# Two layer norms in a transformer block: the Newton chain for the reciprocal root on VectorE instead of GpSimd

## The reference

```python
def layernorm(x): return (x - mean(x)) / sqrt(var(x) + 1e-5)        # over the 512 features
x = x + tanh(g_xattn) * attention(layernorm(x), ctx, ctx, mask)     # 16 heads of 32, with o_proj
h = layernorm(x); h_prev = h moved one row down
xr = mu_r*h + (1-mu_r)*h_prev;  xk = mu_k*h + (1-mu_k)*h_prev
x = x + tanh(g_ffn) * sigmoid(xr @ W_r.T) * (square(relu(xk @ W_k.T)) @ W_v.T)
```

## Time and profile before

| | |
|---|---|
| three runs | 1274.07, 1276.35, 1281.88 us (median 1276.35) |
| profiled execution, span | 1275.5 us; no time outside the span is given for it |
| TensorE matmul | 1184.9 us busy, 93% of the span |
| VectorE | 956.5 us, 75% |
| ScalarE | 763.2 us, 60% |
| GpSimd | 253.7 us, 20% |
| mean granted TensorE clock | 0.977 of full |
| stage 1, the seam, stage 2 | to about 862 us, to 888 us, to the end |

### The profile page before, as it was taken

The page is one execution under the profiler, slowest core; times in us unless marked ns, Lnnn a source line. Parts: engine busy times, 40 slices in busy tenths (PEclk is TensorE's granted clock), DMA queues, the critical chain, the costliest instruction groups (busy, mean ns, idle before and its releaser), DMA issues.

```text
span 1275.5 us, 25860 instructions
## 1 busy us (share of the span) xinstructions
PE 1184.9 (93%) x7424; PEld 933.5 (73%) x7424; DVE 956.5 (75%) x2011; ACT 763.2 (60%) x1632; POOL 253.7 (20%) x427
## 2 busy tenths in 40 slices
PE   3999899999999989999999999987999999999997
PEld 3777676777767767777676777765878878878886
DVE  5778688688778867868877887879677677777763
ACT  4678677678768867867866886774432433343332
POOL 1030030030012003003002100025433443343441
PEclk9999999999999989999998999987999999999999
DMA  6433332253243343233224332461111211211200
GB/s 216 113 96 80 100 108 61 70 143 79 64 125 89 79 98 91 76 99 106 75 59 134 82 83 59 115 196 52 51 50 64 84 49 49 99 49 49 78 37 34
DMA packets 72685, 109.81 MB, mean 86 GB/s; under 512 B 14864, under 2 KB 23696, under 8 KB 72592
## 3 DMA queue, kind: packets, MB, share of 16 engines
q1 hardware_dynamic: 72592, 108.92, 29.9%
HBM read 41.76 MB, written 16.78 MB: 46 GB/s over the span
## 4 chain that ended last, share of the span: by engine, by line
PE 65%; DVE 12%; issue 12%; POOL 6%; ACT 1%; POOLq 1%; DMA 1%; DVEq 1%; SPq 1%; ACTq 0%
PE bank L525 15%; PE bank L461 14%; PE bank L492 11%; PE bank L537 9%; PE bank L518 8%; PE bank L501 6%; DVE xh L992 3%; POOL newton L1094 2%; DVE neg_s L875 2%; PE bank L507 1%; POOL var_eps L1088 1%; DVE stats L832 1%; DVE pT L881 1%; DVE stats L981 1%; POOL rstd L1095 1%
## 5 line engine op out<-in xcount | busy, mean ns | idle before, releaser
L697 ACT ACTIVATE probs<-neg_s,negmax 128x512 f32<-128x512 f32 x512 | 368.3, 721 | 58.6 <-DVE negmax L875 50.5
L875 DVE CUSTOM_DVE_ANT_0 neg_s<-bank,mask_big 128x512 f32<-128x512 f32 x512 | 346.4, 684 | 63.7 <-PE bank L518 36.0
L525 PE MATMUL bank<-ident,probs 128*128 128x128 f32 x2048 | 320.7, 280 | 21.8 <-ACT probs L697 21.3
L525 PEld LDWEIGHTS bank<-ident,probs 128*128 128x128 f32 x2048 | 245.0, 143 | 82.5 <-ACT probs L697 43.0
L518 PE MATMUL bank<-k_stack,q_stack 96*128 96x512 f32 x512 | 247.8, 484 | 15.3 <-DVE negmax L875 15.3
L881 DVE COPY pT<-bank 128x512 f32<-128x512 f32 x256 | 176.5, 690 | 105.8 <-PE bank L525 104.6
L704 ACT COPY pT<-bank 128x512 f32<-128x512 f32 x256 | 149.2, 583 | 107.9 <-PE bank L525 104.1
L1088 POOL TENSOR_SCALAR var_eps<-mv 128x2 f32<-128x2 f32 (+1 forms) x24 | 16.6, 690 | 661.7 <-DVE mv L839 597.5
L537 PE MATMUL bank<-pT,v_sb 128*32 128x512 f32 x1024 | 118.8, 605 | 0.8 <-issue 0.5
L518 PEld LDWEIGHTS bank<-k_stack,q_stack 96*128 96x128 f32 x512 | 99.5, 195 | 22.3 <-DVE negmax L875 10.8
L697 ACT ACTIVATION_READ_ACCUMULATOR probs<-neg_s,negmax 128x1 f32 x512 | 97.0, 190 | 0.0
(11 more groups left out here) (111 smaller groups left out, 2169.5 us busy)
## 6 DMA issues: line engine op xcount, KB each, us to landing
k_stack<-k_hi SPq DMA_DIRECT2D x256, 64.0 KB, 2.0
q_stack<-q_hi SPq DMA_DIRECT2D x256, 64.0 KB, 2.0
x_rows<-x SPq DMA_DIRECT2D x8, 1024.0 KB, 6.9
cT_raw<-ctxT SPq DMA_DIRECT2D x8, 1024.0 KB, 5.5
k_stack<-k_lo SPq DMA_DIRECT2D x128, 64.0 KB, 2.0
q_stack<-q_lo SPq DMA_DIRECT2D x128, 64.0 KB, 2.0
ctx_dram<-ctx_sb SPq DMA_DIRECT2D x32, 256.0 KB, 2.1
c_raw<-ctx_dram SPq DMA_DIRECT2D x16, 512.0 KB, 4.2
```

Source lines behind the costliest of these rows:

```text
L525: mm = nc.tensor.transpose(pt_bank[i % 2][:, a * P:(a + 1) * P], probs[:, i % P_RING, a * P:(a + 1) * P], ident[:])
L697: nc.scalar.activation(probs[:, i % P_RING, :], neg_s[:, i % SM_RING, :], ACT.Exp, bias=negmax[:, k:k + 1], scale=-1.0, accum_out=den[:, g ...
L875: nc.vector.tensor_tensor_reduce(neg_s[:, i % SM_RING, :], s_bank[i % S_BANKS][:], mask_big[:, q, :], 1.0, 3e38, ALU.add, ALU.min, negmax[ ...
```

## The change

`inverse_root` goes from GpSimd's list to VectorE's, with the same 15 links in the same form, and is called at the end of `mean_and_variance` and of `residual1`, behind a wait for the last variance. GpSimd's `normalise` waits for the end of the chain and then writes the rows; `normalise(0)` and `inverse_root2` are gone from its list. VectorE waits at its very start until GpSimd has preset the counters. No tile, matmul or DMA changes.

```diff
         @block.vector
+            def inverse_root(base, sem_, var, ve, y, t):
+                n = [0]
+                def link(ins):
+                    n[0] += 1
+                    ins.then_inc(sem_, 1)
+                    dve.wait_ge(sem_, base + n[0])
+                    apart(dve)
+                link(nc.vector.tensor_scalar(ve, var, EPS, None, ALU.add))
+                link(nc.vector.tensor_scalar(t.bitcast(I32), ve.bitcast(I32), -0.5, RSQRT_MAGIC, ALU.mult, ALU.add))
+                link(nc.vector.tensor_copy(y, t))
+                for _ in range(NEWTON):
+                    link(nc.vector.tensor_tensor(t, y, y, ALU.mult))
+                    link(nc.vector.tensor_tensor(t, t, ve, ALU.mult))
+                    link(nc.vector.tensor_scalar(t, t, -0.5, 1.5, ALU.mult, ALU.add))
+                    link(nc.vector.tensor_tensor(y, y, t, ALU.mult))
...
             def mean_and_variance(b):
...
+                dve.wait_ge(mv_done, b * TT + TT)
+                apart(dve)
+                inverse_root(b * CHAIN, rstd_chain, mv[:, :, 1], var_eps[:], rstd[:], newton[:])
...
+            dve.wait_ge(counters_set, 1)
             for t in range(TT):
                 row_stats(0, t)
...
             def residual1(b, h):
...
+                dve.wait_ge(mv2_done, u * UM + UM)
+                apart(dve)
+                inverse_root(u * CHAIN, rstd_chain2, mv2[:, :, 1], var_eps2[:], rstd2[:], newton2[:])
...
         @block.gpsimd
+            pool.sem_inc(counters_set, 1)
             def normalise(b):
-                pool.wait_ge(mv_done, (b + 1) * TT)
+                pool.wait_ge(rstd_chain, (b + 1) * CHAIN)
                 apart(pool)
-                inverse_root(b * CHAIN, pool_chain, mv[:, :, 1], var_eps[:], rstd[:], newton[:])
...
-            normalise(0)
...
-            def inverse_root2(b, h):
-                u = b * 2 + h
-                pool.wait_ge(mv2_done, (u + 1) * UM)
-                apart(pool)
-                inverse_root(u * CHAIN, pool_chain2, mv2[:, :, 1], var_eps2[:], rstd2[:], newton2[:])
             def step2(b, h):
                 u = b * 2 + h
-                if not (h and is_last(b)):
-                    inverse_root2(*((b, 1) if h == 0 else (b + 1, 0)))
...
             split_w2(1)
-            inverse_root2(0, 0)
             split_w2(2)
```

More of the change, by code:

```diff
@@ L209, in build @@
         small_ld, bias_ld, bv_ld = sem("small_ld"), sem("bias_ld"), sem("bv_ld")
-        unused = sem("unused")
+        unused, counters_set = sem("unused"), sem("counters_set")
         ident_ld = sem("ident_ld")
@@ L217, in build @@
         x_ld, c_ld = sem("x_ld"), sem("c_ld")
-        bn_done, mv_done, pool_chain, xhat_done = sem("bn_done"), sem("mv_done"), sem("pool_chain"), sem("xhat_done")
+        bn_done, mv_done, rstd_chain, xhat_done = sem("bn_done"), sem("mv_done"), sem("rstd_chain"), sem("xhat_done")
         side_mm, side_hi, side_done = sem("side_mm"), sem("side_hi"), sem("side_done")
@@ L229, in build @@
         o_mm, x1_done, bn2_done, mv2_done = sem("o_mm"), sem("x1_done"), sem("bn2_done"), sem("mv2_done")
-        pool_chain2, xh_done, t_mm, xT_done, carry_done = (
-            sem("pool_chain2"), sem("xh_done"), sem("t_mm"), sem("xT_done"), sem("carry_done"))
+        rstd_chain2, xh_done, t_mm, xT_done, carry_done = (
+            sem("rstd_chain2"), sem("xh_done"), sem("t_mm"), sem("xT_done"), sem("carry_done"))
         diff_done, mix_done, mixhi_done, mixlo_done = sem("diff_done"), [sem("mixk"), sem("mixr")], [
@@ L898, in _ @@
                 if kind == "K":
-                    dve.wait_ge(pool_chain, CHAIN)
+                    dve.wait_ge(rstd_chain, CHAIN)
                     for t in range(TT):
@@ L985, in residual1 @@
                     nc.vector.bn_aggr(mv2[:, m, :], stats2[:, m, :]).then_inc(mv2_done, 1)
+                dve.wait_ge(mv2_done, u * UM + UM)
+                apart(dve)
+                inverse_root(u * CHAIN, rstd_chain2, mv2[:, :, 1], var_eps2[:], rstd2[:], newton2[:])
             def normalise2(b, h):
                 u = b * 2 + h
-                dve.wait_ge(pool_chain2, (u + 1) * CHAIN)
+                dve.wait_ge(rstd_chain2, (u + 1) * CHAIN)
                 dve.wait_ge(t_mm, u * UM)
@@ L1077, in _ @@
                 pool.sem_inc(signal, DMA_HEAD)
[L1078 to L1085, removed]
-                    apart(pool)
[L1088 to L1095, removed]
+            pool.sem_inc(counters_set, 1)
             def normalise(b):
-                pool.wait_ge(mv_done, (b + 1) * TT)
+                pool.wait_ge(rstd_chain, (b + 1) * CHAIN)
                 apart(pool)
-                inverse_root(b * CHAIN, pool_chain, mv[:, :, 1], var_eps[:], rstd[:], newton[:])
-                if isinstance(b, int):
-                    return
                 for t in range(TT):
```

## The result

The changed kernel takes 1387.9 us (median of 4 runs, 1385.2 to 1389.1), the kernel before 1277.4 beside it: a ratio of 1.086 [1.083, 1.089], 110 us slower. The profiled execution spans 1387.1 us against 1275.5. The total is the forecast one. The parts are not quite, and two of the errors cancelled; that is what the experiments had to sort out.

A forecast was written before the change was run, and what follows sets the result against it. TensorE was taken to pace both stages, waiting for `xh` in stage 2. Stage 2 72, stage 1 31, seam 6 and start 2 gave 111 us on the profiled 1275.5, hence 1387; range 1300 to 1405.

The forecast's parts named there:

- The bound of before: TensorE paces both stages; in stage 2 it waits for `xh` once a unit, 15 times, 21.4 us in all.
- the term removed: Stage 2: the late GpSimd `add_bias` no longer holds `xh` back, a gain of 1.5 us in each of 14 units.
- A link of 0.30 us: Chain on VectorE: 0.30 us a link, read from the gap between mean and variance; 15 links make 4.6 us.
- the rival of links without cost for the semaphore: Whole kernel: a link is its instruction alone, 0.17 us, the chain 2.6, total 1278 us; chance 0.10.
- A late link held: Stage 2: `add_bias` starts between two links and stops the next; `mix_r_lo` 4.9 us late, v projection 3.4 later.
- The clock: TensorE drops to 1.2 GHz after the new waits in stage 2: 1.5 us in 14 units, 0.7 in the last.
- Stage 1, group 0: Chain delays `rden_rep`, 3.2 us late for TensorE; with 1.2 for the clock, 7 batches x 4.4 = 31 us.
- the row normalisation would hold `rden_rep`: Stage 1: GpSimd's row normalisation, 2.07 us an instruction, starts ahead of `rden_rep`, which then ends at 174.4.
- Seam and start: Seam: GpSimd's split and `add_bias` stall the chain's two-input links, net +6 us; start: `wk_lo` begins later, +2 us.

The follow-up runs named there:

- the last version: The kernel before, chain on GpSimd, with two Newton steps for three and twenty unused-semaphore increments ahead of VectorE's loop: 1254.3 us, 0.981 of before.

## Why the prediction was right, and where it was wrong

- **The bound of before, and the term removed.** Right, shown by the run without the addition: 1.5 us a unit.
- **A link of 0.30 us.** Right: 0.31, of which 0.11 is the separate semaphore instruction, shown by the run without it. The gap between mean and variance was the right row to read it from, and the rival of links without cost for the semaphore fell with it.
- **A late link held.** Right in place and price: twelfth or thirteenth in 13 of 14 units, for 2.1 to 2.4 us. The wait was taken too small: 4.9 for a measured 5.0 to 5.6. Two small terms make it up. Between the end of `mix_r_lo` and the first matmul lie 0.10 us in one unit and 0.24 in the next, which the forecast left out; and from the last variance to `mix_r_lo` it is 6.75 to 7.05 us for 6.8.
- **The clock.** Mechanism right, size wrong: 1.5 us in 14 units were taken from a 3.4 us stretch behind a wait of 2.76; behind the changed kernel's waits of 5 us and more 3.7 to 5.0 us of the work are at the lower level, and that costs 1.8 to 2.4. With the longer wait this makes 1.1 us more a unit. Counted to the transposes of `xh`, the first unit costs 7.9 from the end of `c_lo` on, 13 more cost 6.05 each, and the last one 3.2: 89.6 us for 72.
- **Stage 1, group 0.** The 31 us are met by 30.6, but not by the forecast's parts. The step that fell is that the row normalisation would hold `rden_rep`; in its place the chain keeps VectorE for 5.2 us, not 4.7, so that TensorE waits 2.9 for a forecast 3.2. Each batch costs 2.9 at full clock, and the clock 1.4 a batch in the mean for 1.2; in one of the seven batches it does not fall. (By the forecast's own rows a held copy would end at 174.7 and not at 174.4: GpSimd's first instruction ends at 174.27, and the copy's own 0.43 follow.)
- **Stage 1, the turns.** Missed altogether: -16 us. The two pauses were in the trace of before, but the prediction looked for what the chain waits for and delays, not for where its code puts the loop. That the head's place removes a pause is shown; how much of the 16 is its work is not settled: the turns fell by 6 in the run that only moves it and by 10.5 in the last version, which has the same twenty increments there.
- **Seam and start.** Both agree within 1 us, but the start scatters by more than that, so its 1.1 us show little. The seam's price was two held links, 4.23 and 2.15. The forecast had two-input links stand still there; the two that did are the first two, and each reads one tensor.

So the direction was earned, by a wait that took the place of the one removed. The closeness of the total was luck: the sum's own errors were +18 and -16.

## What to carry to other kernels

A dependent chain of tiny instructions costs its gaps as much as its instructions (0.15 and 0.16 us a link here): count the semaphore instructions between the links, and ask which bulk instruction is queued behind the chain. The two-input GpSimd instruction met a link, `mix_r_lo`, `xh`, `diff` or `kact_lo` here, by where it stood; choose what it meets by the slack behind it, and follow the whole list behind that instruction, as `diff` taught here. When a change leaves TensorE idle in every unit, price the clock from rows behind an idle of that length: one of 1.8 us cost nothing five times and 1.5 us seven times.

## What the runs showed of the hardware

- A two-input GpSimd instruction held a VectorE link as long as it ran, 2.34 us, also a one-input link (4.23 beside 4.50). A one-input GpSimd instruction of 2.77 us held a link for 0.6 to 0.9 us, and the row normalisation held a one-input copy (`rden_rep`) not at all. And a VectorE instruction that started ahead of GpSimd's was not held, GpSimd's was: the addition took 3.12 and 3.33 us.
- Ahead of stage 2's r projection TensorE kept full clock behind every idle stretch of up to 1.64 us, behind 1.8 us in five of twelve, and behind 2.75 to 5.6 us in one of 64 (3.27 us). The length alone does not decide: behind the 2.9 us of waiting for `rden_rep` it kept full clock in one of seven batches of the changed kernel, and in four of seven with `add_bias` behind `mix_r_lo`.
- At the six turns of stage 1's loop VectorE paused 2.0 to 3.1 us behind the branch, and a second time a few instructions later (1.6 to 3.5 us). A single wait added ahead of the loop, or twelve semaphore increments inside it, left the second pause in place; twenty increments ahead of it removed it and made the first 2.7 to 3.1 us long.
